# Graph network on one core: POOL's gathers and scatters of the edge pass issued in turn, tile by tile

## The reference

```python
i, j = (edge_index[0], edge_index[1])
x_i = x[i]
x_j = x[j]
out_i = act(jnp.concatenate([x_i, edge_attr], -1) @ W).reshape(-1, HEADS, DIM)
out_j = act(jnp.concatenate([x_j, edge_attr], -1) @ W).reshape(-1, HEADS, DIM)
alpha = act((jnp.concatenate([out_i, out_j], -1) * att).sum(-1))
...
alpha = segment_softmax(alpha, i, N_NODES)
msg = out_j * alpha[:, :, None]
aggr = jax.ops.segment_sum(msg, i, num_segments=N_NODES)
```

## Time and profile before

| | |
|---|---|
| median of 3 runs | 18,549.41 us (18,542.3 to 18,572.02) |
| profiled execution: its time, its span | 18,550.5 us, 18,548.9 us |
| PE busy | 40% |
| DVE busy | 47% |
| ACT busy | 21% |
| POOL busy | 69% |
| DMA traffic in the edge pass | about 96 GB/s |

### The profile page before, as it was taken

How to read it: one execution, slowest core, us unless ns; L and a number is a source line. 1 busy time by engine, 2 the same in 40 slices (tenths; PEclk the granted TensorE clock), 3 DMA queues, 4 the chain that set the end, 5 groups by cost and what they waited for, 6 DMA issues and landing times. The chain is left out here.

```text
span 18548.9 us, 171693 instructions
## 1 busy us (share of the span) xinstructions
PE 7439.2 (40%) x31521; PEld 6036.6 (33%) x31521; DVE 8703.8 (47%) x16682; ACT 3923.8 (21%) x6193; POOL 12772.7 (69%) x11561
## 2 busy tenths in 40 slices
PE   1444444444444440455333336333364333333332
PEld 1333333333333330455333332333323333223332
DVE  8566666666666666777422231222222222333334
ACT  5455555555545541011000001000010000000000
POOL 6777777777777771566677761777726777557776
PEclk9777777777777775565555555555555555555555
DMA  0433333333333335566211112111121111111111
GB/s 15 96 96 96 98 99 98 96 96 96 96 96 96 96 91 19 151 174 173 59 26 26 26 24 90 26 26 26 26 77 38 26 26 26 21 42 51 51 51 44
DMA packets 1237090, 1244.37 MB, mean 67 GB/s; under 512 B 701413, under 2 KB 943309, under 8 KB 1236800
## 3 DMA queue, kind: packets, MB, share of 16 engines
q1 hardware_dynamic: 852288, 658.63, 13.5%
q0 software_dynamic: 384640, 584.35, 13.4%
HBM read 934.86 MB, written 303.89 MB: 67 GB/s over the span
## 5 line engine op out<-in xcount | busy, mean ns | idle before, releaser
L1233 POOL DMA_INDIRECT l2s_got<-rel_d,l2s_idx x3232 | 3210.2, 993 | 1797.1 <-POOLq L1230 897.8
L1259 PE MATMUL l2s_ps<-l2s_got,l2s_oh 128*128 128x64 f32 x6464 | 1473.4, 423 | 2756.6 <-PEq L1257 2749.7
L1259 PEld LDWEIGHTS l2s_ps<-l2s_got,l2s_oh 128*128 128x128 f32 x6464 | 1409.3, 330 | 2823.6 <-issue 2823.6
L1233 POOL DMA_INDIRECT l3s_got<-ch_d,l3s_idx x1616 | 1612.8, 998 | 755.5 <-issue 438.5
L619 POOL DMA_INDIRECT edge_gath<-h_d,edge_idx_s x1576 | 1709.3, 1085 | 511.0 <-issue 442.5
L623 POOL DMA_INDIRECT edge_gath<-h_d,edge_idx_d x1576 | 1688.3, 1071 | 480.3 <-issue 479.7
L1233 POOL DMA_INDIRECT l1s_got<-h_d,l1s_idx x1616 | 1613.0, 998 | 551.1 <-issue 438.8
L1044 DVE TENSOR_TENSOR net_acc<-net_acc,l2s_ps 128x64 f32 x3232 | 715.4, 221 | 2698.9 <-DVEq L1281 1702.2
L631 POOL DMA_INDIRECT rows_d<-edge_rows,edge_place x1576 | 1640.1, 1041 | 480.0 <-issue 460.9
L764 DVE SCALAR_TENSOR_TENSOR edge_rows<-edge_z,edge_soft 128x1024 f32<-128x1024 f32 x784 | 952.2, 1215 | 2109.6 <-DVEq L762 2109.5
L698 PE MATMUL edge_z<-edge_w_i,edge_in_i 128*128 128x256 f32 x3140 | 1309.7, 506 | 744.6 <-PEq L727 431.8
(11 more groups left out here) (308 smaller groups left out, 15294.5 us busy)
## 6 DMA issues: line engine op xcount, KB each, us to landing
at_rows<-rows_d SPq DMA_DIRECT2D x444, 528.0 KB, 4.1
edge_srow<-in_src SPq DMA_DIRECT2D x197, 512.0 KB, 4.4
edge_lrow<-lo_d SPq DMA_DIRECT2D x197, 512.0 KB, 5.3
rel_d<-l2t_out SPq DMA_DIRECT2D x100, 768.0 KB, 3.3
l2s_got<-rel_d,l2s_idx POOLq DMA_INDIRECT x3232, 2.4
edge_in_i<-in_edge_t SPq DMA_DIRECT2D x197, 256.0 KB, 3.5
edge_in_j<-in_edge_t SPq DMA_DIRECT2D x197, 256.0 KB, 4.1
l1s_got<-h_d,l1s_idx POOLq DMA_INDIRECT x1616, 2.4
```

The costliest lines, as they stand in the source:

```text
L1233: pool.indirect_dma_start(out=got[r][:, j, 0:cols], out_offset=None, in_=table, in_offset=bass.IndirectOffsetOnAxis(ap=idx[i][:, k:k + 1], ...
L1259: ins = pe.matmul(ps[q][:, j, 0:wide], oh[q][:, j, :], got[r][:, j, 0:wide], start=True, stop=True)
```

## The change

POOL's body issues the same 24 DMAs of a group in another order. It waits for `idx_ready`, issues the gathers of tiles 0 and 1, waits for `rows_ready`, and then alternates: the scatter of tile j, and the two gathers of tile j+2 while there are any. The group gathered and the group scattered are the same ones as before, as are all buffers, semaphores and their counts. The first group's gathers ahead of the loop and the last group's scatters behind it are unchanged in order. No other engine's program changes.

```diff
-            def gather(q):
-                pool.wait_ge(idx_ready, 1).then_inc(idx_ready, -1)
-                for j in range(G):
-                    pool.indirect_dma_start(
-                        out=gath[q][:, j, 0:D], out_offset=None, in_=net.h0_d,
-                        in_offset=bass.IndirectOffsetOnAxis(ap=idx_s[q][:, j:j + 1], axis=0)
-                    ).then_inc(gathered[q], 16)
-                    pool.indirect_dma_start(
-                        out=gath[q][:, j, D:2 * D], out_offset=None, in_=net.h0_d,
-                        in_offset=bass.IndirectOffsetOnAxis(ap=idx_d[q][:, j:j + 1], axis=0)
-                    ).then_inc(gathered[q], 16)
-
-            def scatter(q):
-                pool.wait_ge(rows_ready, 1).then_inc(rows_ready, -1)
-                for j in range(G):
-                    pool.indirect_dma_start(
-                        out=net.rows_d, out_offset=bass.IndirectOffsetOnAxis(ap=place[q][:, j:j + 1], axis=0),
-                        in_=rows[q][:, j, OUTJ:OUTJ + ROW], in_offset=None).then_inc(scattered[q], 16)
-
-            gather(0)
+            def fetch(q, j):
...
+            def store(q, j):
...
+            pool.wait_ge(idx_ready, 1).then_inc(idx_ready, -1)
+            for j in range(G):
+                fetch(0, j)
             with Loop(nc, pool, GROUPS):
                 for q in TWO:
-                    gather(1 - q)
-                    scatter(1 - q)
-            scatter(1)
+                    pool.wait_ge(idx_ready, 1).then_inc(idx_ready, -1)
+                    fetch(1 - q, 0)
+                    fetch(1 - q, 1)
+                    pool.wait_ge(rows_ready, 1).then_inc(rows_ready, -1)
+                    for j in range(G):
+                        store(1 - q, j)
+                        if j + 2 < G:
+                            fetch(1 - q, j + 2)
+            pool.wait_ge(rows_ready, 1).then_inc(rows_ready, -1)
+            for j in range(G):
+                store(1, j)
```

More of the change, by code:

```diff
@@ L628, in scatter @@
-            def scatter(q):
-                pool.wait_ge(rows_ready, 1).then_inc(rows_ready, -1)
-                for j in range(G):
-                    pool.indirect_dma_start(
-                        out=net.rows_d, out_offset=bass.IndirectOffsetOnAxis(ap=place[q][:, j:j + 1], axis=0),
-                        in_=rows[q][:, j, OUTJ:OUTJ + ROW], in_offset=None).then_inc(scattered[q], 16)
-            gather(0)
+            def fetch(q, j):
+                pool.indirect_dma_start(
+                    out=gath[q][:, j, 0:D], out_offset=None, in_=net.h0_d,
+                    in_offset=bass.IndirectOffsetOnAxis(ap=idx_s[q][:, j:j + 1], axis=0)
+                ).then_inc(gathered[q], 16)
+                pool.indirect_dma_start(
+                    out=gath[q][:, j, D:2 * D], out_offset=None, in_=net.h0_d,
+                    in_offset=bass.IndirectOffsetOnAxis(ap=idx_d[q][:, j:j + 1], axis=0)
+                ).then_inc(gathered[q], 16)
@@ L636, in _ @@
+            def store(q, j):
+                pool.indirect_dma_start(
+                    out=net.rows_d, out_offset=bass.IndirectOffsetOnAxis(ap=place[q][:, j:j + 1], axis=0),
+                    in_=rows[q][:, j, OUTJ:OUTJ + ROW], in_offset=None).then_inc(scattered[q], 16)
+            pool.wait_ge(idx_ready, 1).then_inc(idx_ready, -1)
+            for j in range(G):
+                fetch(0, j)
             with Loop(nc, pool, GROUPS):
                 for q in TWO:
-                    gather(1 - q)
```

## The result

The changed kernel takes 19,696.58 us (median of 4 runs, 19,675.32 to 19,716.14) against 18,555.79 us of the kernel before on the same chip: a ratio of 1.061, with an interval of 1.0597 to 1.0623. The profiled execution's span is 19,673.7 us, 1,124.8 more than before. Forecast were 19,780 us and a range of 19,410 to 20,060.

What follows compares the result with a forecast made beforehand. POOL, timed by spacing of DMA starts, was taken as the bound at 33.0 us a group. After: 30.5 + 8.8 = 39.3 us, 6.3 more; over 195 periods 1,228 us onto 18,550.5 gives 19,780 us, range 19,410 to 20,060.

Steps and rivals of the forecast that it cites:

- circle through `idx_ready`: POOL's next group waits for ACT's signal, which needs all 16 gathers landed and transposed; 8.8 us from last gather.
- Cover: Behind POOL's last gather two scatters, 2.5 us, remain to hide 8.8 us; POOL idles about 6 us a group.
- Landing: From the end of the last gather's issue on POOL to PE's first transpose: 2.1 us.
- First to last gather: POOL's stretch of now 22 DMAs in a group, taken as 30.5 us.
- price of alternation: POOL switching between gathers and scatters: 0.09 us for each of six more alternations, 0.5 us a group.
- long DMAs: POOL DMAs lengthened as DVE begins L779, four times a group; count left at about 3 to 4 a group.
- Costed at nothing: Waits at `rows_ready` (16 us to spare) and `rows[q]`, PE's own group and SP's loads: no added time.
- A: Last gathers land later behind scatter traffic, 3.5 us against 2.1: period 40.7 us, 20,050 us; chance 8%.
- rule on completions: Skill page: a completion is written only after every earlier write of that DMA engine, over all its queues.
- B: Each turn from gathers to scatters on POOL costs 0.73 us: period 43.1 us, 20,520 us; chance 4%.
- C: No change: 6 us of POOL's period is slack, waits hidden in issue gaps; 18,550 us stays; chance 3%.
- D: Faster: alternation takes POOL out of step with DVE's L779, removing long DMAs; 30.7 us, 18,100 us; chance 2%.

Runs made afterwards that it cites:

- block order: Changed kernel with scatters 0 to 5 in one block between gathers of tiles 0-1 and 2-7, scatters 6-7 last: 19,709.99 us, 1.0597 against the kernel before.
- early `ids`: ACT issues node numbers one group earlier: on the changed kernel 18,551.58 us, on the kernel before 18,512.68 us; ratios 0.9972 and 0.9976 to the kernel before.

## Why the prediction was right

*What bounds the kernel.* Right: POOL by the spacing of its starts, and the circle through `idx_ready` close behind. The block order and the early `ids` show the circle to be the whole of the loss.

*Cover.* Forecast were 8.8 us from last gather to next first gather, with 2.5 covered and some 6 of idle time; measured are 6.0 idle. The parts: from `turn` to `ids` 5.22 us, and 6.51 with the table load, 0.83 to POOL's start, as read before. Landing is the one term a little too large, and there was luck in it: 2.1 us was taken from one group, while the mean of the trace before was 2.5, which would have made 39.7 us and some 19,860. The mean after is 1.9.

*First to last gather.* Forecast 30.5 us, measured 30.14. The price of alternation was set too high: a first scatter costs 1.00 as said, but the gathers behind it 0.96 and 0.94 instead of 0.98 and 0.96, so 0.05 for each alternation instead of 0.09 where nothing else lengthens it. With the circle cut, all six together add 0.05 us to the period (32.80 against 32.75). First to last gather and the 8.6 us behind make 38.76 instead of 39.3 us, and 1,141 us by the runs' medians instead of 1,228.

*The long DMAs.* Their number was rightly left alone, or nearly: 3.9 a group after and 3.6 before. Their cause was wrong: L779 only happened to begin as they should have ended. It is L775 and its two operands in SBUF. In the sum this changed nothing, since L775 too is issued four times a group whatever POOL does.

*Costed at nothing.* `rows_ready` cost nothing in the changed kernel (gaps of 0.3 us, and 15.5 us to spare where 16 were forecast). SP's loads did move out of the way.

*The rivals.* A, late landing, did not come: 1.9 us with a scatter issued just ahead. Of the rule on completions that stood beside it these rows show nothing for a scatter ahead of the last gathers; where SP's loads were issued 1 to 3 us ahead of the gather's end, before and with four scatters behind, the landing was 1 to 2 us longer. B, 0.73 us for each turn, is refuted by the block order, C by the waits. D fell by the condition it was given, a way of 2.8 us where 8.6 were measured; nor did the long DMAs go away. Timing POOL by spans would have given no change; the spacing gave the answer.

## What to carry to other kernels

On an engine that issues for two purposes, find what the next round waits for, and count how much unrelated work stands behind the last instruction that feeds it. That work is the cover of the circle, and spreading it evenly removes it. Before reordering the busy engine, ask if the signal can be raised earlier: here two copies on ACT, moved one group ahead, made the order indifferent. Then look what the next wait has to spare: at `rows_ready` it fell from 15.5 to 3.9 us. And where GpSimd issues DMAs back to back, try one operand of VectorE's large two-input instructions in PSUM, if a bank can be had; here that gave 2.2%.

## What the runs showed that was not expected

A scatter or gather of POOL that starts during a VectorE multiplication of two SBUF tiles ended some 0.8 us after that multiplication, 0.67 us late where it started 0.3 to 0.5 us into it; with one operand in PSUM the same instruction, still 1.22 us long, held up none, and the kernel gained 2.2%. The landing of a gather goes with the place of SP's broadcast loads of 512 KB: 1.7 us on average (from the 60th group on) where they are issued 5 us or more ahead of its end, 2.7 at 2.8 us ahead, and 3.8 for the 47 gathers of the kernel before whose load came 1 to 2 us ahead, as in the earlier trace rows.
